# A macaron block with causal attention on one core: ScalarE takes the accumulator out of PSUM, VectorE turns it from SBUF two tiles later, and the value products stand first in a tile

## The reference

```python
x = x + 0.5 * ffn(layernorm(x), ...)            # 8 experts, top 2
q, k, v = split(layernorm(x) @ w_qkv.T)         # 16 heads of 16
logits = (q @ k.T) / sqrt(16), causal mask
out = softmax(logits) @ v                       # heads side by side
x = x + out @ w_out.T
x = x + 0.5 * ffn(layernorm(x), ...)
```

## Time and profile before

| | us |
|---|---|
| median of 3 executions | 2133.67 (2131.3 to 2133.72) |
| the profiled execution, device time | 2135.9 |
| its span, first to last instruction | 2134.2 |
| TensorE matmul busy | 2052.1 (96%) |
| VectorE busy | 1823.5 (85%) |
| ScalarE busy | 1572.2 (74%) |
| GpSimd busy | 519.0 (24%) |
| mean granted TensorE clock | 0.976 |

### The profile page before, as it was taken

The page is one execution under the profiler, slowest core; times in us unless marked ns, Lnnn a source line. Parts: engine busy times, 40 slices in busy tenths (PEclk is TensorE's granted clock), DMA queues, the critical chain, the costliest instruction groups (busy, mean ns, idle before and its releaser), DMA issues.

```text
span 2134.2 us, 100745 instructions
## 1 busy us (share of the span) xinstructions
PE 2052.1 (96%) x43655; PEld 1616.3 (76%) x43659; DVE 1823.5 (85%) x4023; ACT 1572.2 (74%) x3183; POOL 519.0 (24%) x1298
## 2 busy tenths in 40 slices
PE   5999989999999999999999999999999999979998
PEld 3888865487877878778787787877877777758885
DVE  6766666899999999999999999999999995676665
ACT  5344446598988888888888888888888888334442
POOL 1333213322122221222212213122131211023330
PEclk8899989999999999999999999999999999979998
DMA  8211103311010010100101001010010100331112
GB/s 273 78 47 49 36 30 117 127 29 26 12 34 14 24 30 8 34 15 22 30 8 34 16 23 33 5 33 20 19 34 4 34 4 24 99 117 46 45 49 87
DMA packets 97940, 94.52 MB, mean 44 GB/s; under 512 B 44180, under 2 KB 86936, under 8 KB 97496
## 3 DMA queue, kind: packets, MB, share of 16 engines
q0 software_dynamic: 41376, 42.91, 7.7%
q1 hardware_dynamic: 55776, 45.15, 6.7%
q10 hardware_dynamic: 344, 0.01, 0.0%
HBM read 62.24 MB, written 25.43 MB: 41 GB/s over the span
## 4 chain that ended last, share of the span: by engine, by line
PE 80%; DVE 14%; issue 3%; ACT 1%; POOL 1%; DMA 1%; SPq 1%; ACTq 0%; DVEq 0%; POOLq 0%
PE bank L1236 34%; PE bank L1229 20%; PE bank L1111 17%; DVE work L1744 7%; PE bank L1318 2%; PE bank L1122 1%; PE bank L1347 1%; DVE stats L1377 1%; PE bank L1279 1%; PE bank L1129 1%; DVE rows L1399 1%; DVE x_res L1697 1%; DVE work L1761 0%; SPq L677 0%; DVE work L1740 0%
## 5 line engine op out<-in xcount | busy, mean ns | idle before, releaser
L943 ACT ACTIVATE feat<-bank 128x512 f32<-128x512 f32 (+3 forms) x2304 | 1243.6, 564 | 159.0 <-PE bank L1236 61.7
L1236 PE MATMUL bank<-work 96*32 96x512 bf16 (+2 forms) x15872 | 1227.3, 371 | 12.1 <-DVE work L1744 7.4
L1744 DVE TENSOR_REDUCE work<-bank 128x1 f32<-128x512 f32 (+1 forms) x1920 | 1169.1, 660 | 35.4 <-PE bank L1236 32.4
L1229 PE MATMUL bank<-feat,phase 128*17 128x128 f32 (+3 forms) x18432 | 894.1, 263 | 0.9 <-issue 0.9
L1229 PEld LDWEIGHTS bank<-feat,phase 128*17 128x17 f32 x18432 | 629.9, 98 | 230.5 <-issue 3.2
L1236 PEld LDWEIGHTS bank<-work 96*32 96x32 bf16 (+1 forms) x15872 | 483.6, 96 | 79.9 <-DVE work L1744 56.7
L1111 PE MATMUL bank<-work 128*128 128x256 f32 (+1 forms) x1872 | 394.9, 361 | 0.4
L1111 PEld LDWEIGHTS bank<-work 128*128 128x128 f32 x1872 | 322.5, 190 | 35.9 <-DVE work L1628 0.6
L618 POOL TENSOR_SCALAR_AFFINE_SELECT feat<-feat 128x128 f32<-128x128 f32 x512 | 148.3, 293 | 367.6 <-ACT feat L943 346.2
L556 POOL DMA_INDIRECT work<-token_table,row_no x142 | 138.4, 974 | 290.0 <-PE bank L1122 142.7
L1628 DVE COPY work<-phase 128x514 f32 x234 | 101.4, 436 | 122.1 <-ACT work L857 98.3
(11 more groups left out here) (201 smaller groups left out, 1380.7 us busy)
## 6 DMA issues: line engine op xcount, KB each, us to landing
phase<-in_w SPq DMA_DIRECT2D x12, 1024.0 KB, 12.0
work<-qk_parts POOLq DMA_DIRECT2D x60, 192.0 KB, 3.6
token_table<-rows SPq DMA_DIRECT2D x8, 1056.0 KB, 8.7
work<-work SPq DMA_DIRECT2D x512, 0.5 KB
qk_parts<-phase SPq DMA_DIRECT2D x20, 384.0 KB, 2.8
work<-qk_parts POOLq DMA_DIRECT2D x60, 128.0 KB, 3.8
qk_parts<-work SPq DMA_DIRECT2D x12, 384.0 KB, 2.6
x_res<-in_x SPq DMA_DIRECT2D x8, 512.0 KB, 7.7
```

The lines of the kernel that those rows point to most:

```text
L943: eng.activation(p_ring[:, n % P_RING, lo:QB], s_bank("probs", n)[:, lo:QB], ACT.Exp, scale=HD ** -0.5).then_inc(sig.s_done, 1)
L1229: mm = eng.matmul(bank[ACC_BANK][GRID * g:GRID * g + VW, GRID * i0:P], v_aug[:, t, h, :], weights[:, i0:TPJ, g, :], start=(t == 0), stop=( ...
L1236: mm = eng.matmul(out[GRID * g:GRID * (g + 1), width], left[:, GRID * g:GRID * (g + 1)], right, start=start, stop=stop)
L1744: eng.tensor_reduce(maxima[:, h % 2, j, PLACE[i], at:at + 1], scores[:, 0:hi - lo], AX_X, ALU.max).then_inc(sig.a_done, 1)
```

## The change

There are four edits, all in attention.

1. At `"acc"` ScalarE copies bank 5 (128 by 128, fp32) into a new buffer `acc_out` in SBUF, two deep, which lies in a part of `feat` that the ring of exponentials leaves free. VectorE's transpose is a new step `"turn"`, two tiles later (`TURN_LAG`); it reads `acc_out` and no longer bank 5. `"divide"` comes two tiles after `"turn"`. The next unit's first value product waits for ScalarE's copy.
2. Within a tile the value products (and `"acc"`) come ahead of the probability product, behind the scores.
3. The pause after a unit's last value product is one tile (`PV_PAUSE` 2 to 1).
4. `"unit_max"` comes two scores after the unit's last one. `"max_row"` stays four scores after it.

Two semaphore arrays are merged into one, to make room for the new semaphore `acc_turned`. The number of matmuls is the same. The diff, without the renamed semaphores:

```diff
@@ -82,9 +82,9 @@
 SPLIT_BF, SPLIT_F = 5, 3
 LEAD = 44 * QB
 MAX_RING = 4
-PV_LAG, PV_PAUSE, DIVIDE_LAG = 5, 2, 2
+PV_LAG, PV_PAUSE, TURN_LAG, DIVIDE_LAG = 5, 1, 2, 2
 GRID = 32
-MAX_ROW_LAG = 4
+UNIT_MAX_LAG, MAX_ROW_LAG = 2, 2
 
 LOAD_PIECES = [(part, c, half) for part in range(len(K_PARTS)) for c in range(2) for half in range(2)]
 LOAD_FIRST, LOAD_EVERY = 24, 5
...
@@ -167,19 +167,24 @@
             ended += 1
     yield "end_chunk", ended
     ended += 1
-    a, a_done, b_done, u, unsent = 0, 0, 0, 0, []
-    summed, pause, undivided = 0, 0, []
-    for n in range(ITEMS):
-        while a < len(A_ITEMS) and a_done < b_done + LEAD:
+    a, a_done, used, u, unreduced, unsent = 0, 0, 0, 0, [], []
+    summed, pause, unturned, undivided = 0, 0, [], []
+
+    def due_scores():
+        nonlocal a, a_done, u, begun, ended
+        while a < len(A_ITEMS) and a_done < used + LEAD:
             h, j, i, k = A_ITEMS[a]
             yield "scores", a
             lo, hi = keys_of(j, i, k)
             a_done += hi - lo
             a += 1
             if a == len(A_ITEMS) or A_ITEMS[a][:2] != (h, j):
-                yield "unit_max", u
-                unsent.append((a + MAX_ROW_LAG, u))
+                unreduced.append((a + UNIT_MAX_LAG, u))
                 u += 1
+            while unreduced and (unreduced[0][0] <= a or a == len(A_ITEMS)):
+                n = unreduced.pop(0)[1]
+                yield "unit_max", n
+                unsent.append((a + MAX_ROW_LAG, n))
             while unsent and (unsent[0][0] <= a or a == len(A_ITEMS)):
                 yield "max_row", unsent.pop(0)[1]
             if ended < begun:
...
@@ -188,6 +193,22 @@
             if a % CHUNK_EVERY == 0 and begun < len(CHUNKS):
                 yield "begin_chunk", begun
                 begun += 1
+
+    def width_of(n):
+        h, j, t = B_ITEMS[n]
+        return QB - max(t - TPJ * j, 0) * P
+
+    def probs(n):
+        nonlocal used
+        h = B_ITEMS[n][0]
+        piece, between = divmod(n - PER_HEAD * h - LOAD_FIRST, LOAD_EVERY)
+        if h < H - 1 and between == 0 and 0 <= piece < len(LOAD_PIECES):
+            yield "load_stack", (h + 1, piece)
+        yield "probs", n
+        used += width_of(n)
+
+    for n in range(ITEMS):
+        yield from due_scores()
         while ended < len(CHUNKS):
             if begun > ended:
                 yield "end_chunk", ended
...
@@ -195,13 +216,9 @@
             if begun < len(CHUNKS):
                 yield "begin_chunk", begun
                 begun += 1
-        h, j, t = B_ITEMS[n]
-        piece, between = divmod(n - PER_HEAD * h - LOAD_FIRST, LOAD_EVERY)
-        if h < H - 1 and between == 0 and 0 <= piece < len(LOAD_PIECES):
-            yield "load_stack", (h + 1, piece)
-        yield "probs", n
-        b_done += QB - max(t - TPJ * j, 0) * P
-
+        while unturned and unturned[0][0] <= n:
+            yield "turn", unturned[0][1]
+            undivided.append((n + DIVIDE_LAG, unturned.pop(0)[1]))
         for _ in range(0 if pause else 2):
             if summed > n - PV_LAG:
                 break
...
@@ -210,9 +227,10 @@
             summed += 1
             if t == TPJ * (j + 1) - 1:
                 yield "acc", h * NJ + j
-                undivided.append((n + DIVIDE_LAG, h * NJ + j))
+                unturned.append((n + TURN_LAG, h * NJ + j))
                 pause = PV_PAUSE + 1
                 break
+        yield from probs(n)
         pause = max(pause - 1, 0)
         while undivided and undivided[0][0] <= n:
             yield "divide", undivided.pop(0)[1]
...
@@ -220,7 +238,10 @@
         yield "pv", summed
         summed += 1
     yield "acc", len(UNITS) - 1
-    for _, u in undivided + [(ITEMS, len(UNITS) - 1)]:
+    for _, u in unturned + [(ITEMS, len(UNITS) - 1)]:
+        yield "turn", u
+        undivided.append((ITEMS, u))
+    for _, u in undivided:
         yield "divide", u
 
 
...
@@ -301,7 +321,7 @@
         self.causal, self.divided = one("causal_zeros"), one("divided")
         self.unseen = one("unseen_lowest")
         self.recip = one("recip")
-        self.pv, self.acc = one("pv"), one("acc_copied")
+        self.pv, self.acc, self.turned = one("pv"), one("acc_copied"), one("acc_turned")
         self.heads_tr, self.heads_copy = one("heads_tr"), one("heads_copied")
         self.out_mm, self.attended = one("out_mm"), one("x_attended")
 
...
@@ -427,6 +447,8 @@
         recip = carve(2 * TPJ).rearrange("p (b i) -> p b i", b=2)
         sums = carve(2 * TPJ * GRID).rearrange("p (b i w) -> p b i w", b=2, i=TPJ)
         p_ring = feat[:, :, :].rearrange("p k s -> p (k s)")[:, 0:P_RING * QB].rearrange("p (r s) -> p r s", r=P_RING)
+        spare = feat[:, :, :].rearrange("p k s -> p (k s)")[:, P_RING * QB:]
+        acc_out = spare[:, 0:2 * P].rearrange("p (b s) -> p b s", b=2)
         v_aug = phase[:, 0:NT * H * VW].rearrange("p (i h w) -> p i h w", i=NT, h=H)
         at_v = NT * H * VW
 
...
@@ -942,6 +964,11 @@
                         need.wait_ge(sig.proj, KD * len(CHUNKS))
                         eng.activation(p_ring[:, n % P_RING, lo:QB], s_bank("probs", n)[:, lo:QB], ACT.Exp,
                                        scale=HD ** -0.5).then_inc(sig.s_done, 1)
+                    elif what == "acc":
+                        h, j = UNITS[n]
+                        need.wait_ge(sig.pv, pv_at[unit_end(h, j)])
+                        need.wait_ge(sig.turned, n - 1)
+                        eng.activation(acc_out[:, n % 2, :], bank[ACC_BANK][:, 0:P], ACT.Copy).then_inc(sig.acc, 1)
 
             def copy_heads(n):
                 need.wait_ge(sig.pv, PV_ALL)
...
@@ -1754,14 +1781,13 @@
                         need.wait_ge(sig.max_row[n % MAX_RING], 16 * TPJ * (n // MAX_RING))
                         eng.transpose(max_rows[:, n % MAX_RING, :],
                                       max_cols[:, n % MAX_RING, :]).then_inc(sig.max_turned, 1)
-                    elif what == "acc":
-                        h, j = UNITS[n]
-                        need.wait_ge(sig.pv, pv_at[unit_end(h, j)])
+                    elif what == "turn":
+                        need.wait_ge(sig.acc, n + 1)
                         need.wait_ge(sig.divided, n - 1)
                         eng.transpose(sums[:, n % 2].rearrange("p i w -> p (i w)"),
-                                      bank[ACC_BANK][:, 0:P]).then_inc(sig.acc, 1)
+                                      acc_out[:, n % 2, :]).then_inc(sig.turned, 1)
                     elif what == "divide":
-                        need.wait_ge(sig.acc, n + 1)
+                        need.wait_ge(sig.turned, n + 1)
                         need.wait_ge(sig.divided, n - 1)
                         eng.reciprocal(recip[:, n % 2, :], sums[:, n % 2, :, HD]).then_inc(sig.recip, 1)
 
```

More of the change, by code:

```diff
@@ L260, in __init__ @@
         self.const = one("constants")
-        self.x_loaded = many("x_loaded", NT // LN_GRP[0])
+        self.block_loaded = many("token_block_loaded", NJ)
         self.gate_pad, self.small = one("gate_padded"), one("small_loads")
@@ L293, in __init__ @@
         self.stack, self.stack_ones = many("stack_loaded", 2), one("stack_ones")
-        self.first_stack = many("first_stack_block", NJ)
         self.a_full, self.a_done = one("a_full"), one("a_done")
@@ L677, in load_first_stack @@
                         eng.dma_start(stack[r * HD:(r + count) * HD, 0, c, block],
-                                      src).then_inc(sig.first_stack[sc], 16)
+                                      src).then_inc(sig.block_loaded[sc], 16)
                     r += count
@@ L682, in _ @@
                 a, b = g * LN_GRP[0], (g + 1) * LN_GRP[0]
-                eng.dma_start(x_res[:, a:b, :], x_rows[:, a:b, :]).then_inc(sig.x_loaded[g], 16)
+                eng.dma_start(x_res[:, a:b, :], x_rows[:, a:b, :]).then_inc(sig.block_loaded[g], 16)
             load_experts(0)
@@ L1211, in stack_ready @@
                     for sc in range(j + 1):
-                        need.wait_ge(sig.first_stack[sc], 96)
+                        need.wait_ge(sig.block_loaded[sc], 16 + 96)
                 else:
@@ L1371, in statistics @@
                     if n == 0:
-                        need.wait_ge(sig.x_loaded[g], 16)
+                        need.wait_ge(sig.block_loaded[g], 16)
                     elif n == 1:
```

## The result

| | before | after |
|---|---|---|
| median, us | 2133.69 (2131.3 to 2134.83, 6 executions) | 2120.72 (2118.73 to 2127.47, 6 executions) |
| ratio, 95% interval | | 0.995 [0.9936, 0.9963] |
| the profiled execution, us | 2135.9 | 2123.74 |
| its span, us | 2134.2 | 2122.0 |
| TensorE, VectorE, ScalarE busy, us | 2052.1, 1823.5, 1572.2 | 2044.4, 1817.9, 1597.6 |

The change makes the kernel faster by 0.5%: 13.0 us by the medians, 12.2 by the profiled executions, 7.9 to 13.7 by the interval of the ratio. Forecast were 9.2 us and 2124.7; the range (2120 to 2133) held, by 0.7 us at its lower end.

The account below looks back on a forecast made before the run. TensorE's matmuls were taken to bound attention, leaving only its waits to gain. The terms, -9.7 + 0.5 = -9.2 us, rounded to -9, took the median of 2133.67 to 2124.7 us, with an 8 in 10 range of 2120 to 2133.

Parts of the forecast that it names:

- What bounds the kernel: In attention: TensorE's matmuls bound it, busy 1387.8 of 1397.3 us; only time TensorE loses waiting can be gained.
- rival C: Weight loads in attention: their 46.9 us of waits for the maxima are all TensorE loss and go, giving 2087; chance 0.03.
- One tile of pause: Scores after a unit's end: gaps of 0.27 us at j = 1 and 0.35 at j = 2 close, saving 9.7 us.
- Turning from SBUF: VectorE's transpose, two tiles later: takes 0.31 us, as from PSUM, and costs TensorE nothing there.
- no other gap that repeats: TensorE's timeline in attention: beyond the places after j = 1 and j = 2, no further repeating gap was found.
- ScalarE's copy: At a unit's end: runs 0.42 to 0.70 us after the last value product, in time by 0.01 to 0.23, costing nothing.
- One sign named in advance: In the profile after: TensorE's value products would show no wait for ScalarE.
- rival A: At a unit's end: TensorE waits for ScalarE's copy; at 0.15 us x 127 = 19 us the time is 2144; chance 0.09.
- Value products first: Within a tile: each value product comes 0.22 us sooner behind its exponential, which is five tiles back; gain 0.
- Unit maximum: VectorE, two scores later: gains about 0.13 us in each of 128 units, 17 us, none of it on the path.
- End of attention: Last exponentials and final chain: one copy adds 0.2 us where ScalarE is the bound, copy and hand-over add 0.3.
- Rival B: In attention: the gaps only move, VectorE being 96% busy; half the gain or less remains, 2130 to 2134; chance 0.15.

Follow-up runs that it names:

- experiment 1: The changed kernel with the pause of two tiles back, all else kept: 2130.97 us, 0.9988 of the kernel before.
- experiment 4: The changed kernel with the unit maximum right behind the unit's last score again, the row still four scores behind: 2123.73 us, 0.995 of the kernel before.
- experiment 6: The kernel before with only ScalarE's copy and the later transpose added: 2129.47 us, 0.9974 of the kernel before.
- 8 with 42 and 43 blocks: The changed kernel with pass A 42 or 43 blocks ahead of pass B, not 44: 2119.24 us (0.9947 of the kernel before) and 2118.83 us (0.995).
- experiment 9: The kernel before with only the value products put ahead of the probability product in a tile: 2132.69 us, 0.9997 of the kernel before.
- experiment 3: The changed kernel with the probability product ahead of the value products in a tile, as before: 2142.11 us, 1.0032 of the kernel before.
- experiment 7: The changed kernel with ScalarE copying the accumulator twice, first into a buffer that nobody reads: 2134.89 us, 1.0 of the kernel before.

## Why the prediction was right, step by step

*What bounds the kernel* held: TensorE, by waits that its starts show and its busy time hides. The weight loads' waits overstated the loss here as they did there. They fell from 46.9 us to 15.6 + 13.7 = 29.3, by 17.6, and the time by 12.2; rival C (2087) had no ground. The Trainium skill (Trainium Kernel Development and Optimization, Best Practices) judges the distance to the roofline by MFU (the share of the peak arithmetic that is reached) and by the busy share of the weight loads. That share went from 78% to 77% (1062 of 1388 us) while the kernel got faster; in this kernel the starts of the matmuls were the better guide.

*One tile of pause, 15 x 0.27 + 16 x 0.35 = 9.7 us.* The gaps measured 0.24 and 0.37 in every head, 9.8 us. The sum is right, the credit only in part. The pause closes the first; copy and pause share the second (experiment 1); and 0.12 of the 0.61 needs the unit's maximum moved as well (experiment 4).

*Turning from SBUF.* The duration was right: 0.30 against the 0.31 from PSUM, so SBUF was no faster. Missed was what else VectorE's transpose held. **The step that failed is "no other gap that repeats": a third one, 0.15 us behind the end of j = 0, was in the trace of before.** 16 x 0.15 = 2.4 us is most of what the result has over the forecast (13.0 against 9.2 by the medians). The interval of the ratio (7.9 to 13.7 us) holds both numbers, so it is the heads that show this and not the times. Every kernel with ScalarE's copy in which that copy was in time or the pause was two tiles closed it (experiments 1, 4, 6, 8 with 42 and 43 blocks); neither kernel without the copy and with two tiles of pause did (before, and experiment 9).

*ScalarE's copy, costed at nothing, with a cover of 0.01 to 0.23 us.* By start and duration: forecast 0.42 to 0.70, measured 0.46 to 0.73. It held, and the cover is as thin as was said: at the narrowest blocks (j = 0, 5, 7) the next value product comes 0.80, 0.80 and 0.78 us on, where 0.77 to 0.79 are free. One sign named in advance did not come as worded: the weight loads of value products do wait for ScalarE, 50 times and 13.7 us in all. It cost the matmuls 0.03 us or less at a unit's end. Experiments 3 and 7 show what rival A would have cost: with 0.22 us of delay the kernel is slower than before, with 0.16 us as fast as before. That the copy was in time by 0.01 us at the narrowest blocks was forecast from single rows read to 0.01 us, so it was in part luck.

*Value products first, costed at nothing.* True alone (experiment 9), and 19 us wrong as a statement on the changed kernel: without this part the copy comes too late (experiment 3). The copy's start was reckoned in the new order, so the sum held.

*Unit maximum, 0.* It gives 0.12 us in a head, 2 us, by what the heads show.

*End of attention, +0.5* (0.2 where ScalarE is the bound, 0.3 for the hand-over). It held. Up to the 111th of the 144 exponentials of head 15 the changed kernel is 0.77 us ahead, as in any head. From there to the last one, by starts, ScalarE took 9.53 us before and takes 9.77 now, +0.24. From the last value product to the first matmul behind attention TensorE went from 1.31 to 1.62 us, +0.3. Comparing head 15 between its neighbours' last value products would hide this: the new order moves those against the exponentials.

*The whole.* The two gaps, the third one and the end give -9.8 - 2.4 + 0.5 = -11.7 us. The prediction was to be wrong "if the time falls by over 13 us", and the medians fell by 13.0: that neither this bound nor the range's 2120 was passed is by less than the spread of the times (2118.7 to 2127.5), and so in part luck.

*Rival B*, the gaps only move: not in the whole change. Parts of it did move them (experiment 6, the end of j = 1).

Put side by side, the parts don't add. Of a head, the copy alone saves 0.23 us, the value products first alone 0.02, the short pause alone costs 0.32: together a loss of 0.07. All in one, the head saves 0.76. The unit's maximum was not tried alone.

Open is what TensorE waits for in the long heads, above all in unit j = 3 of heads 6 and 10. The profile names no releaser, and no experiment was made on it.

## What to carry to other kernels

Where one engine is 96% busy by modelled ends, look for its loss in the distances of starts, and divide the trace by the period of the loop: a median for each unit found a gap of 0.15 us that neither idle time nor waits had named. Then look at what the median leaves out as well, and at whether it comes back at one place. When a change frees a buffer by way of another engine, count which instruction stands ahead of the freeing one on that engine; one group more or less in the order decided between 0.5% faster and 0.3% slower. Parts that each seem worth nothing may be the condition of another, so test them out of the whole change as well as alone.

## What the runs showed of the hardware

A transpose of 32 by 32 blocks of a 128 by 128 fp32 tile takes nearly as long from SBUF as from PSUM: 299 ns after, 306 ns before, as medians of 128 each. ScalarE's copy of that shape takes about what the exponential does:

```profile
L1787 DVE STREAM_TRANSPOSE work<-feat 128x128 f32<-128x128 f32 x128 | 38.3, 299 | 21.7 <-ACT feat L971 21.7
...
L965 ACT ACTIVATE feat<-bank 128x128 f32<-128x128 f32 x128 | 35.9, 281 | 7.9 <-PE bank L1345 0.9
L971 ACT ACTIVATE feat<-bank 128x128 f32<-128x128 f32 x128 | 35.1, 274 | 0.8 <-PE bank L1256 0.8
```

Two such copies in a row start 0.16 us apart (experiment 7, the median of 128 ends, 157 ns) though each lasts 0.27, so the second one cost ScalarE a little more than half of its duration. TensorE's weight loads followed the instruction that released them, on VectorE or ScalarE, by 0.05 to 0.06 us at each place read.
